# A graph layer on one core: 49 bins laid out like the nodes, every second group binned, bins added in pairs, three copies of the sums

## The reference, cut to what matters

```
h = relu(layernorm(x))                       # x: 6250 nodes x 64
e = relu(concat(h[dst], edge_attr) @ W1.T + b1)   # 206250 edges, 128 wide
e = relu(e @ W2.T + b2)
summed = segment_sum(e, src)                 # one row of 128 per node
cnt = segment_sum(ones, src)
agg = summed / max(cnt, 1)
z = relu(concat(h, agg, u[0]) @ Wa.T + ba)
out = x + z @ Wb.T + bb
```

## Time and profile before

| | us |
|---|---|
| median of 3 runs (2480.56 to 2488.11) | 2480.77 |
| the profiled execution | 2479.19 |
| its span, first to last instruction | 2477.4 |
| before the first scatter | 133.7 |
| first to last scatter | 2132.1 |
| last scatter's start to the end of the span | 211.6 |

### The profile page before, as it was taken

The page is one execution under the profiler, slowest core; times in us unless marked ns, Lnnn a source line. Parts: engine busy times, 40 slices in busy tenths (PEclk is TensorE's granted clock), DMA queues, the critical chain, the costliest instruction groups (busy, mean ns, idle before and its releaser), DMA issues.

```text
span 2477.4 us, 44859 instructions
## 1 busy us (share of the span) xinstructions
PE 1959.7 (79%) x12527; PEld 1601.6 (65%) x12527; DVE 1268.0 (51%) x4970; ACT 918.5 (37%) x2077; POOL 1875.1 (76%) x1231
## 2 busy tenths in 40 slices
PE   2288777779888888888888888888878888886666
PEld 2166565567676767776676766677766777775554
DVE  5064444446555555555555555555555555542228
ACT  3144443344443444443443433444433444430002
POOL 7768888888888888888888888888888888885000
PEclk8599999989999999999999999999999999985558
DMA  8088888779998989898899888899989998985338
GB/s 313 19 194 153 146 142 144 137 144 190 171 173 176 173 174 186 171 181 166 174 181 178 176 176 173 173 182 184 172 169 176 176 184 174 176 155 107 90 117 286
DMA packets 405652, 416.99 MB, mean 168 GB/s; under 512 B 52368, under 2 KB 304176, under 8 KB 404784
## 3 DMA queue, kind: packets, MB, share of 16 engines
q1 hardware_dynamic: 241280, 338.13, 48.4%
q0 software_dynamic: 163008, 74.84, 33.7%
q10 hardware_dynamic: 1120, 1.11, 0.1%
HBM read 231.43 MB, written 182.44 MB: 167 GB/s over the span
## 4 chain that ended last, share of the span: by engine, by line
POOL 53%; issue 21%; PE 16%; DVE 5%; DMA 3%; ACT 1%; POOLq 0%; DVEq 0%; ACTq 0%; SPq 0%
POOL sums L705 42%; POOL sums L693 8%; PE bank L1178 6%; PE bank L1127 2%; PE bank L1140 2%; DMA sums<-regA,idx 2%; PE bank L1116 2%; PE bank L1104 2%; DVE regC L986 1%; POOL regC L596 1%; POOL regC L591 1%; DVE regC L1001 1%; PE bank L1138 1%; ACT h L808 1%; DMA sums<-regB 0%
## 5 line engine op out<-in xcount | busy, mean ns | idle before, releaser
L705 POOL DMA_INDIRECT sums<-regA,idx x972 | 1531.9, 1576 | 326.5 <-issue 289.3
L1140 PEld LDWEIGHTS bank<-w,h 128*128 128x128 f32 x3224 | 433.6, 195 | 153.0 <-issue 141.6
L1104 PE MATMUL bank<-h,regC 128*128 128x130 f32 x2560 | 359.2, 284 | 112.7 <-ACT h L808 89.4
L1127 PE MATMUL bank<-regA,L 128*128 128x512 f32 x806 | 435.5, 623 | 2.0 <-DVE regA L929 2.0
L794 ACT ACTIVATE regA<-bank 128x516 f32<-128x516 f32 x243 | 146.1, 601 | 780.1 <-DMA sums<-regA,idx 641.2
L1140 PE MATMUL bank<-w,h 128*128 128x128 f32 x3224 | 433.2, 278 | 0.0
L1178 PE MATMUL bank<-regC 128*112 128x129 f32 x2240 | 379.1, 323 | 51.4 <-DVE regC L986 51.4
L1104 PEld LDWEIGHTS bank<-h,regC 128*128 128x128 f32 x2560 | 319.1, 195 | 130.3 <-ACT h L808 102.2
L1178 PEld LDWEIGHTS bank<-regC 128*112 128x112 f32 x2240 | 329.1, 214 | 72.7 <-DVE regC L986 69.4
L936 DVE TENSOR_REDUCE rank<-bank 128x4 f32<-128x224 f32 x160 | 62.7, 392 | 602.7 <-PE bank L1164 485.6
L1116 PE MATMUL bank<-h,regC 128*128 128x129 f32 x1944 | 292.7, 297 | 80.6 <-issue 26.8
(11 more groups left out here) (147 smaller groups left out, 1420.1 us busy)
## 6 DMA issues: line engine op xcount, KB each, us to landing
slots<-regC SPq DMA_DIRECT2D x320, 260.0 KB
regC<-slots SPq DMA_DIRECT2D x280, 260.0 KB
regA<-in_ea SPq DMA_DIRECT2D x202, 256.0 KB
src<-rows_src SPq DMA_DIRECT2D x243, 128.0 KB
dstR<-rows_dst SPq DMA_DIRECT2D x403, 64.0 KB
sums<-regA,idx POOLq DMA_INDIRECT x972
regA<-sums SPq DMA_DIRECT2D x12, 1290.0 KB, 7.1
sums<-zeros SPq DMA_DIRECT2D x20, 645.0 KB, 9.6
```

Of the source, the lines that this page charges most:

```text
L705: nc.gpsimd.indirect_dma_start(out=sums, out_offset=bass.IndirectOffsetOnAxis(ap=idx[:, n % RING, t:t + 1], axis=0), in_=scat[:, n % 4, t, ...
L1104: last = T.matmul(psSlot(t)[:, k, :], place, h2[:, g % 2, t, :], start=True, stop=True)
L1127: T.matmul(psL1(s % 2), L[:, s % RING, :], R[:, s % RING, :], start=True, stop=True).then_inc(l1_done, 1)
L1140: last = T.matmul(psL2(g % 2)[:, t * H:(t + 1) * H], h1[:, g % 2, t * TILE:(t + 1) * TILE], w2[:, :], start=False, stop=t == TPG - 1)
```

## The change

What it does:

- Bins. 49 instead of 56, with 128 columns each instead of 112 (`src` = 49 p + b). The result of a bin then lies as the final stage reads the nodes, so `acc` is added there from SBUF; the fifth copy and its store are gone, and one row per partition fewer is computed (49 of 50).
- Which groups. Every odd group from 3 to 379 but those with g % 24 = 23 from 72 on: 177 binned, 226 plain, 1081 scatters. Groups 380 to 402 are all plain.
- Blocks of 30 (the last of 27) and units of 2 bins: 25 units a block, spread evenly over the steps to the next block, the last block's two a step at steps 387 to 399. A unit's 8 matmuls (16 in the profile) go to one PSUM bank, behind which VectorE adds two bins at once. Where a step has two units, the first stands between the layers. Two unit buffers of 2 bins replace four bin buffers. VectorE makes a unit's 0/1 matrices a step earlier.
- Copies. 3 copies of the sums, each a tensor of its own; scatter n goes to copy n mod 3 (in order of issue) and waits for n-3. 15 zeroing DMAs, the last 4 in steps 1 to 4. Per chunk 3 loads of one copy each.
- Slots. 49 x 4 + 32 = 228 rows a binned group are stored, not 256.
- The check. 192 odd groups instead of 160. GpSimd converts `src` itself and finds bins and digits; VectorE makes the 14 indicator arrays, clips and sums in 12 rounds of two instructions; the bias matmuls are gone. GpSimd takes over the splitting of `b2`, VectorE the addition of `bb` to `x` (at step 200). The array `home` and its tables are gone, since the copy is now chosen by the tensor.

```diff
-NSETS = 4
+NSETS = 3
-ZAFTER = (0, 1, 1, 1, 1, 1, 2, 2)
+ZAFTER = (0, 1, 1, 1, 1)
...
-LAST_SORTED = 400
-NBIN = 56
-LO = 112
+LAST_SORTED = 380
+SKIP_FROM, SKIP = 72, 24
+NBIN = RU
+LO = P
...
-BLOCK = 32
+BLOCK = 30
...
 def is_sorted(g):
-    return 0 <= g < LAST_SORTED and g % PERIOD in SORTED
+    return 2 < g < LAST_SORTED and g % 2 == 1 and not (g >= SKIP_FROM and g % SKIP == SKIP - 1)
...
+def unit_steps():
     at = {}
+    firsts = [block[-1] + VREAD + 1 for block in BLOCKS]
+    for k in range(len(BLOCKS)):
+        for q in range(UNITS):
+            s = firsts[k] + (firsts[k + 1] - firsts[k]) * q // UNITS if k + 1 < len(BLOCKS) else firsts[k] + q // 2
+            at.setdefault(s, []).append((k, q))
     return at
...
-            floored(quot[:, :], srcH[:, :], NBIN)
...
-            for c in range(7):
-                G.tensor_scalar(A2[:, :, c], quot[:, :], float(c), None, ALU.is_equal).then_inc(A12_ready, 1)
...
+            G.tensor_copy(srcF[:, :], srcI[:, :]).then_inc(srcF_ready, 1)
...
+            floored(quots, odd, NBIN)
...
+                if c >= NCH - BA:
+                    dve.wait_ge(digits_ready, 1)
+                    VE.tensor_scalar(A2[:, :, c - NCH + BA], quot, float(c - NCH + BA), None, ALU.is_equal).then_inc(A12_ready, 1)
...
+            for k in range(NPACK // 4):
+                dve.wait_ge(spill_psum, k + 1)
+                wait(dve, spilt_ready, k - 1)
+                VE.scalar_tensor_tensor(out=spill[0:wide, k % 2, :, :], in0=bank[0:wide, 4 + k % 2, 0:4 * wide].rearrange("p (a c) -> p a c", c=wide), scalar=float(CAP),
+                                       in1=same[:, :, :].rearrange("p a c -> p (a c)").unsqueeze(1).broadcast_to([wide, 4, wide]), op0=ALU.max, op1=ALU.mult).then_inc(spill_ready, 1)
...
+            def add_up(k, q, general):
+
+                m, rows = UNIT_NO[k, q], CAP * len(BLOCKS[k])
+                nb = unit_bins(q)[1]
+                pe.wait_ge(oh2_ready, m + 1)
+                wait(pe, acc_ready, m)
+                for i in range(nb):
+                    for t in range(TPG):
+                        last = T.matmul(psUnit[:, i * C:(i + 1) * C], oh2[0:rows, m % 2, i, t, :] if not general else zeros[0:rows, 0:LO],
+                                        BR[0:rows, m % UNIT_RING, i, t, 0:C], start=t == 0, stop=t == TPG - 1)
+                last.then_inc(unit_done, 1)
...
-            sp.wait_ge(acc_ready, len(BIN_NO))
-            sp.dma_start(sums[NSETS * NROWS:NSETS * NROWS + LO * NBIN, :].rearrange("(p b) c -> p (b c)", b=NBIN), acc[0:LO, :, :].rearrange("p b c -> p (b c)")).then_inc(acc_stored, 16)
...
+                    for k in range(NSETS):
+                        sp.dma_start(SA[:, c % NACC, k, 0:(r1 - r0) * C], sums_v[k][:, r0 * C:r1 * C]).then_inc(acc_in[c % NACC], 16)
...
-                    VE.tensor_tensor(s1[:, :, 0:m * C], SA[:, s, 0:2, 0:m * C], SA[:, s, 2:4, 0:m * C], ALU.add).then_inc(s1_done, 1)
+                    link(VE.tensor_tensor(s1[:, 0:m * C], SA[:, s, 0, 0:m * C], SA[:, s, 1, 0:m * C], ALU.add))
+                    link(VE.tensor_tensor(s2[:, 0:m * C], s1[:, 0:m * C], SA[:, s, 2, 0:m * C], ALU.add))
+                    VE.tensor_tensor(s2[:, 0:m * C], s2[:, 0:m * C], acc[:, r0:r1, :].rearrange("p r c -> p (r c)"), ALU.add).then_inc(s2_done, 1)
```

More of the change, by code:

```diff
@@ L17 @@
 NROWS = P * RB
+RU = -(-N // P)
+NKEPT = P * RU
 RCH = 4
@@ L88, with mid_unit, end_unit, arrived @@
 SCATTER, SCATTERS = scatter_table()
-def bin_steps():
+def unit_steps():
     at = {}
[L93 to L97, removed]
-    return at
[L101 to L105, removed]
+    firsts = [block[-1] + VREAD + 1 for block in BLOCKS]
[3 more added lines that the diff above has]
+            at.setdefault(s, []).append((k, q))
+    return at
+UNITS_AT = unit_steps()
+STEPS = max(max(UNITS_AT) + 2, NG + VSUM + 1)
+CONSTS = 16
+DERIVED = 8
+XBB_STEP = 200
+UNIT_NO = {kq: n for n, kq in enumerate(kq for s in sorted(UNITS_AT) for kq in UNITS_AT[s])}
+def mid_unit(s):
+    return UNITS_AT[s][:-1] if s in UNITS_AT else []
+def end_unit(s):
+    return UNITS_AT[s][-1:] if s in UNITS_AT else []
+def arrived(m):
+    order = sorted(UNIT_NO, key=UNIT_NO.get)[:m + 1]
+    return sum(unit_bins(q)[1] for n, (_, q) in enumerate(order) if n % UNIT_RING == m % UNIT_RING)
+def unit_bins(q):
+    return PAIR * q, min(PAIR, NBIN - PAIR * q)
+assert LO * NBIN == NKEPT >= N and P < SLOTS <= PW and NG + max(VSUM, VLAG) < STEPS and LAST_SORTED <= 2 * ODD
+assert NBIN == BA * BA and PACK * BA <= P and NS % (4 * PACK) == 0 and max(len(u) for u in UNITS_AT.values()) <= 2
 def build(nc, x, src_cols, dst_cols, src_rows, dst_rows, ea, u, w1t, b1, w2t, b2, wat, ba, wbt, bb, out):
@@ L115, in build @@
     table = nc.dram_tensor("p_table", (NROWS, H), f32, kind="Internal").ap()
-    sums = nc.dram_tensor("sums", ((NSETS + 1) * NROWS, C), f32, kind="Internal").ap()
+    sums = [nc.dram_tensor(f"sums{k}", (NROWS, C), f32, kind="Internal").ap() for k in range(NSETS)]
     rows_src = nc.dram_tensor("rows_src", (P * GPP, GE), u16, kind="Internal").ap()
@@ L1133, in step @@
                         last.then_inc(l1_done, 1)
+                for k, q in mid_unit(s):
+                    add_up(k, q, general)
                 g = s - 1
@@ L1170, in step @@
                     T.matmul(psOver, prefix[:, :], over[:, n % 2, :], start=True, stop=True).then_inc(over_done, 1)
-                for k, b in BINS_AT.get(s, ()):
-                    m, rows = BIN_NO[k, b], CAP * len(BLOCKS[k])
-                    pe.wait_ge(oh2_ready, m + 1)
-                    wait(pe, acc_ready, m if k + 1 < len(BLOCKS) else m - 3)
-                    if k + 1 == len(BLOCKS) and b == 0:
-                        pe.wait_ge(h2_ready, NG)
-                    for t in range(TPG):
-                        last = T.matmul(psBin(k, m), oh2[0:rows, m % 2, t, :] if not general else zeros[0:rows, 0:LO], BR[0:rows, m % BIN_RING, t, 0:C], start=t == 0, stop=t == TPG - 1)
-                    last.then_inc(bin_done, 1)
+                for k, q in end_unit(s):
+                    add_up(k, q, general)
             general = pe.value_load(mode[0:1, 0:1], min_val=0, max_val=1)
@@ L1194, in z_of_h @@
                     w, q = (r1 - r0) * P, (r1 - r0) // 2
-                    for s in range(2):
+                    for s in range(min(2, RU - r0)):
                         z_half = psZ(n)[:, 0:w].rearrange("p (q s e) -> p q s e", q=q, s=2)[:, :, s, :]
```

333 lines of the change are left out of this document (163 added, 170 removed).

## The result

The changed kernel took 2414.4 us (median of 4 runs, 2404.5 to 2420.1) against 2480.7 us (4 runs): a ratio of 0.972, 95% interval 0.970 to 0.974. It is faster by 66 us, where I had forecast 261, and it lies above the range of 2160 to 2305.

What follows compares the result with a forecast made beforehand. It took GpSimd, issuing scatters without a pause, as the bound. Start 80.5, scatters 2035.8, landing waits 40 and end 61.5 sum to 2218 us of span, 2220 of time; range 2160 to 2305.

Steps and rivals of the forecast that it cites:

- Three copies: Scatter loop: each scatter waits for the third before it; taken at 0.04 us each, 40 us, with bounds nothing and 216 us.
- leaves 5.55 us from start to landing: Scatter loop with three copies: time a scatter may take to land without delay, at the bare pace of 1.55 + 0.30.
- the two rows: Two scatters in the old profile, read as landing by 4.8 and 5.65 us; one of two called 0.1 us too late.
- Rival 3: Scatter loop: landings grow to 6.0 us on average, pace 2.0 us, +84 us, 2304 us in all; chance 0.11.
- TensorE 3.84 + 2 x 1.8 at most: Last 23 plain groups: TensorE's time a step against GpSimd's 7.5 us, so the last block's bins lie under GpSimd's work.
- The start, 80.5: Before the loop: first scatter at 80.5 us, 53 us earlier, with 14 indicator arrays at 0.8 us and twelve rounds.
- TensorE in the binned stretch: Binned steps: TensorE needs 117 us for 24 steps, GpSimd 119, so about level; costed at nothing.
- Rival 2: Binned stretch: TensorE sets the pace as its clock drops, +106 us to 2326, or halfway 2270; chance 0.17.
- The scatters' own pace: Scatter loop: 1081 scatters instead of 1132, 1080 intervals of 1.885 us, 2035.8 us, 96 less.
- The end, 61.5: After the last scatter: 4.8 us to land, 4.5 for the first load, 52.2 of VectorE's chain; 150 us less.
- rival 4: Scatter loop: slower than before, gain gone at a pace of 2.16 us, landings of 6.5 us; chance 0.02.
- rival 5: Change fails its aim: other loop version runs, +3039 us, or last bins end behind the last scatter, up to 166; chance 0.02.

Runs made afterwards that it cites:

- experiment 1: Changed kernel with a fourth copy of the sums, zeroed in the loop: 2281.7 us, ratio 0.919 to the kernel before.
- after: The changed kernel itself, with three copies and the last block's pairs of bins two a step: 2414.4 us, ratio 0.972 to the kernel before.
- experiment 4: Changed kernel with both four copies of the sums and the last block's pairs of bins one a step: 2208.5 us, ratio 0.890 to the kernel before.
- experiment 2: Changed kernel, three copies, with the last block's pairs of bins one a step (steps 387 to 411): 2349.5 us, ratio 0.946 to the kernel before.
- experiment 5: Kernel before the change, four copies kept, each scatter also waiting until the third before it has landed: 2691.2 us, ratio 1.083.
- experiment 7: As experiment 4, with GpSimd's operations on b2 waiting until VectorE has made the 14 digit arrays: 2209.5 us, ratio 0.890 to the kernel before.
- experiment 6: As experiment 4, with each scatter also waiting until the second before it has landed: 2990.7 us (one run).

## Why the prediction was wrong

Two steps failed, and between them they hold 179 of the 185 us that the sum was short.

**Three copies, "I take 0.04 each, 40 us": a term mis-sized.** The mechanism was right, the wait for n-3, and so was the place. The price was 133 us (experiment 1 against after) to 141 (experiment 4 against 2), 0.12 to 0.13 an interval of the 1080, inside the bound of 0.2 that I had kept, but three times the value taken. (The fourth copy's own 12 us, at a zeroing and at the end, are in these differences; the intervals of the middle alone give 0.134 and 0.149.)

Part of the error is in "leaves 5.55 us from start to landing". That is from start to start. A waiting scatter starts 0.27 us after the landing, so the landing must come within about 5.28 us. ScalarE's copy in turn starts 0.10 us after it in the median, so the two rows put the landings at 4.7 and 5.55, and the second is 0.27 us too late and not 0.1. Half of 0.27 is 0.135, which is the measured price; from two rows that is luck.

The other part is that two rows at one place don't show a distribution. The trace of the kernel before holds it: 233 of ScalarE's 239 copies started within 8 us of the last scatter that they had to wait for, 4.99 us after it on average with 6.5 at the 95th per cent. But 63 of these the profile puts down to TensorE's product, so that the landing was earlier; the 164 put down to a landing have 4.83 on average and 6.3 at the 95th per cent. The mean of what lies beyond the allowance, 5.38 us to ScalarE's start, is 0.20 over all 233, and 0.08 if only the 164 count as late at all. The measured 0.134 lies between these two bounds, and the trace gives no more than the bounds (the 0.157 of experiment 5's expectation counts all 233 against 5.56). The mean alone would have said that nothing is lost.

Rival 3's pace of 2.0 was the one that came (2.027), though it needed no growth of the landings: experiment 5 has the price without any of the change's traffic, and experiment 1 runs at a share of 0.93 with 18 us of landing waits.

**"TensorE 3.84 + 2 x 1.8 at most", and so the last bins cost nothing: wrong.** It is a sum of busy times. With two pairs a step, two buffers, one bank and VectorE's program order, each step's end is tied to the next by the ring of 17.11 us, of which TensorE's products are the smaller part. It cost GpSimd 82 us of waiting, 65 us of the time (experiment 2) or 73 (experiment 4 against 1). 82 us in 13 waits is 78 net of 0.3 each, which is the tail's 76. The condition "under GpSimd's 7.5 us a step" was right, and one a step meets it: the tail took 174.3 us in experiment 4.

**The start, 80.5: 8 us short.** GpSimd had the digits at 38.15 us, where 38 was worked out, but by luck: the conversion took 1.57 us and not 4.6, and the ten operations 25.1 and not 22. VectorE's twelve rounds took 1.18 us each (1.25). The arrays failed: 14 x 0.8 was scaled from an operation that writes its elements side by side, and these write one element in seven. (That this is the reason is not shown; the output's type differs too.) The seven of L912 took 1.54 us each, those between the table's rows 1.6 to 2.6, and the last was ready at 60.5, not 52. Experiment 7 shows that this is their own price and not GpSimd's doing. The `b2` work on GpSimd changed nothing, as forecast: it was over at 62.4 us, while VectorE was still in its rounds (61.3 to 75.6 us).

**TensorE in the binned stretch, costed at nothing: right.** With four copies the pace was 1.893 at a clock of 0.98 and TensorE busy 89%. Rival 2 is out, and its condition went the other way: the clock rose from 0.95, and TensorE's busy share from 83% (1751 of 2098 us).

**The scatters' own pace, 1081 at 1.885: right within 1%** (1.893 and 1.896 with hardly any landing waits left, 8 to 11 us in the middle's 977). **The end, 61.5: right** (59.7; 3.3 us to the first load's issue instead of 4.8, 5.0 to VectorE instead of 4.5, 51.3 behind it instead of 52.2). Rivals 4 and 5 did not come: the pace stayed under rival 4's 2.16, the first version of the loop ran, and no stretch behind the last scatter was left but the end.

My own bound for being wrong was a mean interval over 2.0; it was 2.088. Of GpSimd's waits for its own scatters I had forecast 10 to 80 us; they were 206. The ranges of the unknown terms were in the text, 216 us for the copies and the last bins' 166 in rival 5; the mistake in the numbers was to give rival 3 11 in 100 on two rows, and to the last bins nothing between "hidden" and "all behind".

## What to carry to other kernels

Before a ring is made shorter, take every wait in the trace that shows when its entries come free, leave out those that something else ended, take off what passes between the release and the start that waits for it (0.27 us here), and price the mean excess over what is then allowed. A few rows at one place don't show the tail of a distribution. And an experiment that adds a wait to a kernel can add a price of its own: here 0.7 us from landing to start in place of 0.27. Before work is hidden under another engine at a higher rate per step, walk its dependency ring once round (free buffer, load, indicator, products, addition, the other work in program order between them) and compare the ring, not the busy times, with the step. And when two shortfalls are found, try both repairs together: here they added to 206 us and turned a gain of 2.8% into 11.0%.

## What the runs showed of the hardware

- **A scatter-add lands under 4.9 us after its start on average** with scatters 1.9 us apart (ScalarE's 233 copies in the kernel before, 4.99 less 0.10) and under 4.7 with 2.63 us between them (experiment 6). Both are upper bounds. The pace by copies was 1.89 us (four, GpSimd's own), 2.03 (three) and, with the price of an added wait in it, 2.63 (two).
- **From the landing to the start of the scatter that waits for it:** 0.27 us in 192 of 198 waits of the changed kernel; 0.7 us in 294 of 412 in experiment 6, where a wait of its own stands between the two.
- **The same sixteen matmuls at two speeds within a step:** 3.78 us behind a pause of 7.87 us and 1.95 us some microseconds later, the rows of the tail above. The granted clock was 0.50 from 2188.5 to 2192.3 us and 1.00 from 2193.8 to 2195.6. The difference, 1.8 us, is a part of the ring's 17.11. The granted clock of the tail of the changed kernel (2105 to 2300 us) averaged 0.71.

```profile
2105.00:2300.00 195.00, 102.39 (x595) 93.77 (x606) 58.13 (x189) 22.37 (x39) 97.59 (x61) 0.71 0.52 95
```

- **GpSimd beside VectorE's row of bf16 arrays stood for 12.13 us on an operation of 0.60 us** and ended 0.14 us after VectorE's last; VectorE lost nothing (experiment 7): its seven arrays took 10.77 us with GpSimd at work beside them and 10.79 without. What held GpSimd up is not shown.
- **An operation that writes one element in seven** took VectorE 1.54 us for 768 elements (f32 to bf16), 2.0 ns each, where the earlier trace rows had 512 side by side (bf16 to f32) in 509 ns, 1.0 ns each. Whether the step or the types double it was not tried.
